# A four-layer transformer chain on one core: waiting for each part of a product's input instead of for all four

## The reference

```python
# L0: adaptive RMS norm, rotary attention (8 query heads of 64, one key/value head), silu-gated MLP of 2048
h = ada_rms(x, time_emb, ln1_w, ln1_tw); x = res + ctx @ Wo.T
h = ada_rms(x, time_emb, ln2_w, ln2_tw); x = res + silu(h @ Wg.T) * (h @ Wu.T) @ Wd.T
# L1: layer norm with scale and shift, cosine attention (16 heads of 32), gelu MLP of 2048
x = x + attn(_ln(x) * (scale1 + 1.0) + shift1) * gamma1
x = x + (gelu((_ln(x) * (scale2 + 1.0) + shift2) @ Wfc1.T + bfc1) @ Wfc2.T + bfc2) * gamma2
# L2: layer norm, sparse masked attention with a 128-wide latent for keys and values
out = y @ Wo.T; x = x + out
# L3: 8 expert MLPs (64 -> 256 -> 64), layer norm, silu, 512x512 product
proj = silu(hn) @ out_W + out_b; return x + proj
```

## Time and profile before

| | |
|---|---|
| median of 3 runs | 2081.14 us (2078.93 to 2084.55) |
| the profiled execution | 2079.02 us, span 2077.1 us |
| PE busy | 1904.8 us, 92% |
| DVE, ACT, POOL busy | 1114.6, 1027.6, 790.3 us |
| PE's granted clock, mean | 0.965 of 2.4 GHz |
| moved by DMA | 314.84 MB, mean 152 GB/s |

### The profile page before, as it was taken

How to read it: one execution, slowest core, us unless ns; L and a number is a source line. 1 busy time by engine, 2 the same in 40 slices (tenths; PEclk the granted TensorE clock), 3 DMA queues, 4 the chain that set the end, 5 groups by cost and what they waited for, 6 DMA issues and landing times.

```text
span 2077.1 us, 35268 instructions
## 1 busy us (share of the span) xinstructions
PE 1904.8 (92%) x12880; PEld 1507.4 (73%) x12880; DVE 1114.6 (54%) x3184; ACT 1027.6 (49%) x2473; POOL 790.3 (38%) x1094
## 2 busy tenths in 40 slices
PE   4789999999999999999899999989999989978977
PEld 3567777888778878887778777868876768755565
DVE  5756444644553365345664676574554675456353
ACT  3543323433343354443555465555567466368665
POOL 4555652211114242234667454326332432233220
PEclk9999999999999999999999999989999989989989
DMA  7235767555445445444345434523434425322311
GB/s 265 89 127 193 239 223 266 200 193 188 162 163 178 158 139 178 158 145 165 129 171 185 152 127 138 184 102 113 152 112 142 157 77 187 128 77 69 120 62 51
DMA packets 98795, 314.84 MB, mean 152 GB/s; under 512 B 11584, under 2 KB 13376, under 8 KB 97088
## 3 DMA queue, kind: packets, MB, share of 16 engines
q1 hardware_dynamic: 98624, 312.58, 43.9%
HBM read 242.55 MB, written 66.58 MB: 149 GB/s over the span
## 4 chain that ended last, share of the span: by engine, by line
PE 73%; DVE 12%; POOL 5%; ACT 5%; issue 4%; DMA 2%; SPq 0%; POOLq 0%; DVEq 0%; ACTq 0%
PE B L190 67%; PE B L193 6%; POOL R L208 2%; DVE FB L211 2%; DVE T L208 2%; DMA ST<-in_wpack 2%; DVE SS L214 1%; ACT FB L196 1%; ACT SS L196 1%; POOL W L208 1%; DVE PT L202 1%; POOL SS L205 1%; DVE FB L208 1%; DVE HA L211 1%; DVE Y L208 1%
## 5 line engine op out<-in xcount | busy, mean ns | idle before, releaser
L205 POOL TENSOR_SCALAR SS<-SS,NM 128x256 f32<-128x256 f32 (+1 forms) x640 | 289.0, 469 | 778.1 <-DVE NM L220 777.8
L190 PE MATMUL B<-HM,W 128*128 128x512 f32 x2304 | 538.3, 394 | 14.7 <-DVE HM L211 8.5
L190 PEld LDWEIGHTS B<-HM,W 128*128 128x128 f32 x2304 | 437.1, 190 | 108.6 <-DVE HM L211 9.4
L190 PE MATMUL B<-G,W 128*128 128x512 f32 x1536 | 394.9, 407 | 17.7 <-DVE G L208 6.0
L190 PEld LDWEIGHTS B<-G,W 128*128 128x128 f32 x1536 | 287.6, 193 | 88.4 <-issue 18.3
L196 ACT ACTIVATE SS<-SS,NM 128x256 f32<-128x256 f32 (+1 forms) x512 | 240.5, 471 | 117.1 <-DVE NM L214 116.5
L190 PE MATMUL B<-HA,W 128*128 128x512 f32 x864 | 222.1, 408 | 11.9 <-DVE HA L208 7.7
L193 PE MATMUL B<-ident,SS 128*128 128x128 f32 x1152 | 177.3, 291 | 36.6 <-POOL SS L205 30.7
L190 PEld LDWEIGHTS B<-HA,W 128*128 128x128 f32 x864 | 166.1, 196 | 49.6 <-DVE HA L208 8.1
L208 DVE TENSOR_TENSOR G<-FB,G 128x512 fp32r<-128x512 f32 x128 | 100.8, 788 | 171.9 <-ACT G L196 171.8
L193 PEld LDWEIGHTS B<-ident,SS 128*128 128x128 f32 x1152 | 128.2, 146 | 72.6 <-issue 44.5
(11 more groups left out here) (108 smaller groups left out, 2651.0 us busy)
## 6 DMA issues: line engine op xcount, KB each, us to landing
W<-kept SPq DMA_DIRECT2D x357, 512.0 KB, 4.2
kept<-W SPq DMA_DIRECT2D x119, 512.0 KB, 4.7
ST<-in_wpack SPq DMA_DIRECT2D x139, 256.0 KB, 2.9
Y<-in_adaw SPq DMA_DIRECT2D x12, 1024.0 KB, 5.9
FB<-FB SPq DMA_DIRECT2D x52, 64.0 KB, 3.0
X<-in_xT SPq DMA_DIRECT2D x1, 3072.0 KB, 14.4
out_xT<-X SPq DMA_DIRECT2D x12, 256.0 KB, 2.1
FB<-in_pos SPq DMA_DIRECT2D x4, 256.0 KB, 4.3
```

The source lines that it names most:

```text
L190: return self.real.matmul(*a, **k) if self.real is not None else self
L205: return self.real.tensor_scalar(*a, **k) if self.real is not None else self
```

## The change

`product` gets an argument `due`. Where it is given, the wait for part i of the input stands right before the three matmuls that read part i. It is given for the attention projections that read HA (the values of layer 1 at L1055 and the products from L2's latent keep theirs), for all `up`, `down` and last products. The waits for weights and bank stay ahead of the first matmul. Two numbers of `PLACE` change as well: the end of MLP 7 and the position of `nsub` in norms with a mean.

```diff
-    "up end": [35.49, 52.243, 66.359, 84.262, 100.699, 123.295, 147.706, 164.324],
+    "up end": [35.49, 52.243, 66.359, 84.262, 100.699, 123.295, 147.706, 163.582],
...
-    "a stats": [0.101, 1.202, 1.481, 1.791, 2.6],
+    "a stats": [0.101, 1.202, 1.42, 1.791, 2.6],
...
-            def product(bank, parts):
+            def product(bank, parts, due=None):
+
+
                 last = len(parts) - 1
                 for i, (w, x) in enumerate(parts):
+                    if due is not None:
+                        e.wait_ge(*due[0].of(*due[1:], i))
                     e.matmul(bank, w[0], x[0], start=(i == 0), stop=False)
...
-                        e.wait_ge(*d_nlo.of(("a", L, n), 3))
+                        due = d_nlo, ("a", L, n)
                     e.wait_ge(*ready(n, *name))
                     e.wait_ge(*dp.over(u))
-                    product(bank[:, :], parts).then_inc(*p_qkv.up(*k))
+                    product(bank[:, :], parts, due).then_inc(*p_qkv.up(*k))
...
-                    e.wait_ge(*d_nlo.of(("m", L, n), 3))
...
-                                                  for kc in range(4)]).then_inc(*p_up.up(q, c, j, x))
+                                                  for kc in range(4)], (d_nlo, ("m", L, n))).then_inc(*p_up.up(q, c, j, x))
...
-                        e.wait_ge(*d_glo.of(q, c, j))
...
-                                              for j in range(4)]).then_inc(*p_down.up(q, c, m))
+                                              for j in range(4)], (d_glo, q, c)).then_inc(*p_down.up(q, c, m))
...
-                    e.wait_ge(*d_nlo.of(("z", h, n), 3))
...
-                                               for c in range(4)]).then_inc(*p_last.up(n, m, h))
+                                               for c in range(4)], (d_nlo, ("z", h, n))).then_inc(*p_last.up(n, m, h))
```

More of the change, by code:

```diff
@@ L1006, in tensor @@
                         w, latent = piece(n, *name), piece(n, *LATENT)
-                        parts = [(part(w, 0, 128), latent)]
+                        parts, due = [(part(w, 0, 128), latent)], None
                         e.wait_ge(*d_ck.of(n))
```

## The result

The changed kernel takes 2062.62 us (median of 4 runs, 2061.08 to 2065.75); the kernel before, run beside it, 2082.85 us (4 runs, 2078.93 to 2085.32). The ratio is 0.9909, 95% interval 0.9889 to 0.9928: faster by 0.9%, some 20 us. The forecast was 2065 with a range of 2055 to 2077. The profiled executions lie 13.2 us apart (spans 2077.1 and 2063.9), since the one of before was near its fastest run and this one is the slowest of its four.

A forecast was written before the change was run, and what follows sets the result against it. PE, busy 1904.8 of 2077.1 us, was taken as the bound. Waits by part (19.8 us) plus places (1.0) made 20.8, times 0.8 gave 16.6 us won: forecast 2065 us, range 2055 to 2077.

The forecast's parts named there:

- What bounds the kernel, and the arithmetic of the gap: PE bounds; nine of twelve matmuls move into a gap, minimum 0.229 us each; idle falls 15 to 20 us.
- The six long waits: PE's six longest waits: 11.0 to 20.7 us won, middle 15.8; lower if the clock rises unchanged, upper if earlier.
- G at 218.57: PE's 2.37 us wait for G nearly closes, its product comes near 3 us: 2.1 to 3.8 us won.
- The two locks by bank: At ("a", 2, 3) and ("z", 2, 2) the first product also awaits its bank: 1.9 to 3.5 and 1.5 to 3.2 us.
- The nine short waits: PE's nine waits of 0.3 to 0.9 us mostly vanish: 3.5 to 4.7 us won, 4.0 taken.
- The places: Moved steps at MLP 7's end, chunks 2 and 3 and some norms: about +1 us together, bounds -3 and +4.
- How much arrives: Share of the 20.8 us reaching the kernel's end: between half and everything, factor 0.8 taken, 16.6 us.
- A: Clock comes back early in all six gaps and the places give their upper bound: 2056 us, chance 0.15.
- B: Bursts of matmuls leave the clock where it was, or it swings: 2069 us, chance 0.16.
- C: Gaps come back downstream, half or less of the gain arrives: 2071 to 2076 us, chance 0.17.
- D: Gaps filled but found again before the next squares or roots, places cost 3 us: 2081 to 2084, chance 0.06.
- E: Each of 171 waits inside products holds back the next load of weights: 2069 to 2097 us, chance 0.04.

The follow-up runs named there:

- eleven traces with four steps: Traces of the changed kernel and variants that wait separately for each of four input parts; the ten kernels' ratios lie between 0.9874 and 0.9910.
- places only: Kernel before with the two new `PLACE` numbers but the old waits: 2080.4 us, ratio 0.9985.
- the three traces of the table: Two traces of the changed kernel and one of the kernel before with waits by part but old places (2061.5 us, ratio 0.9893).
- the second trace: Another trace of the unaltered changed kernel, against the kernel before: 13.4 us gained over all matmuls.
- the end alone: Changed kernel with `nsub` put back at its old position, so waits by part and the new MLP 7 end: 2060.62 us, ratio 0.9899.
- the two kernels with the cover kept: Changed kernel with old `nsub` position and MLP 7 end at 164.1; one also waits for `down` weight pieces by part: 2059.15 and 2060.36 us.
- the second measurement of the two kernels: Changed kernel run again, unaltered, as yardstick against the kernel before on one chip: 2058.72 us, ratio 0.9881.
- the two-step kernel: Changed kernel with parts 0 to 2 all waiting for part 2 and part 3 for itself: 2067.08 us, ratio 0.9912.

## Why the prediction was right, point by point

**What bounds the kernel, and the arithmetic of the gap: right.** PE's idle time fell by 17.0 us where 15 to 20 were forecast; over the eleven traces with four steps it is 150.1 to 159.3 us, 13 to 22 less. The waits left by name are 7.5 us; with the two that the bank now ends (2.5 at ("a",2,3) and 4.6 at ("z",2,2)) they are 14.6, at the low end of the 14 to 20.

**The six long waits: right in sum, wrong in two of its terms.** 3.6 + 3.4 + 1.1 + 2.6 + 1.2 + 1.5 = 13.4 us against a middle of 15.8, inside 11.0 to 20.7. Its lower bound, 0.229 per moved matmul, rested on the clock rising at the same moment as before. It did not: at ("m",0,0) nothing behind the last part was left at the lower clock, so that gap gave its upper bound, in all eleven traces with four steps. At ("a",0,0) seven or eight matmuls moved, as forecast, and the gain was mostly over the upper bound of 3.1 (2.6 to 4.4 us in these traces; 0.7 in places only, where nothing moved, is the noise of such a figure). Where the pauses stay (("m",1,0)) the clock rose 1.3 us sooner, and the gap gave 2.6, 1.5 and 2.0 us, about its lower bound of 2.1, in the three traces of the table; over all eleven it is 1.4 to 3.6, and more where the clock came back sooner. So both bounds were met in this gap, and what decides between them from one execution to the next is open. The terms below their lower ends are G at 218 us and ("a",2,3), next.

**G at 218.57: right where it arises, wrong downstream.** The product came to 2.96 us as forecast and 3.2 us were won, in the range of 2.1 to 3.8. But 1.1 (or -0.6 in the second trace) are left at 230 us. The step that failed is "all other waits of PE (softmax rows, sums of squares, reciprocal roots, weights, banks) stay as they are": a wait for weights that had been hidden behind the wait for G came out two steps later.

**The two locks by bank: right.** The first product behind ("a",2,3) and ("z",2,2) starts with the bank, not with part 0. PE of the changed kernel, with releasers that are the scalings, as the earlier trace rows said:

```profile
1837.05 4.57 PE L190 MATMUL B<-HA,W 128*128 128x512 f32 x12 [2.47 <-DVE FB L211]
...
1982.50 0.77 PE L190 MATMUL B<-ZH,W 128*128 128x512 f32 x1 [4.63 <-DVE FB L208]
```

These two gave 1.2 and 1.5 us, below and at their lower ends (1.9 and 1.5): behind the bank nearly all of the product is at the lower clock (4.57 us for 12, 4.36 before). That is not so in every order: with the end alone and in the two kernels with the cover kept, ("a",2,3)'s product takes 3.0 us and the gap gives 2.5; in the other eight traces it gives 1.1 to 1.7.

**The nine short waits: right.** The five that I can follow singly gave 1.0, 1.1, 1.0, 0.6 and about 0.8 us (1670 to 1690), 4.5 together, where 4.0 were forecast for all nine. One of them, at 165 us, was lost again: `few,T` and the scores behind it then waited 0.19 and 1.95 us (the latter 1.41 before).

**The places: inside the bounds, but with the wrong sign.** +1 forecast, with bounds of -3 and +4; in the trace -1.2 at ("a",2,0), +1.2 at `nvar`, +1.2 at chunk 3 and about -2.7 behind it, some -1.5. The first is as forecast. At `nvar` only the idle time counts: the kernels that leave `nvar` where it was gained 1.5 there too. The product behind it takes 4.20 us in the trace of before and 3.0 in all five others that have it there, so the share of the clock was not the place's. The term that was missing is the last one. The working had asked what the moved steps meet at their new place, and not what stood at the place they left: a 3 us `down` that covered a softmax. That accounts for 1.1 us of it; the rest is the slow product behind. By the medians the places are worth nothing either way. This is the sort of step that one has to look for in the order.

**How much arrives: not confirmed.** Of the 20.8 us of the sum 16.6 were to arrive. It was 13.2 in the profiled pair, 20.2 in the medians, and 27.2 in the medians of the second measurement of the two kernels, which is over the whole sum. The range held all of these; the factor 0.8 fits neither median. The factor was to stand for DVE not following; what took gain away in the traces are weights at 190 to 230 us, the softmax rows at 1810 us, and spells of low clock which differ by 4 us and more from one execution to the next. In those the pair of traces is misleading: PE's busy time is 1902.1 to 1911.1 us in kernels that do the same matmuls.

**The rivals.** A (2056) is half there: the clock came early in the gap that closed, not in those with pauses. B (2069) is out as an account of the whole: the first two gaps gave more than their lower bounds (3.6 and 3.4 against 1.7), and the bursts beat the single start of the two-step kernel. Its lower bounds held at ("z",2,2) and nearly at ("m",1,0). C is true of single gaps (165, 212 us) and not of the whole. D and E are out: idle time fell and did not come back, and waits cost nothing that shows. E's range was also summed wrongly: 20 to 32 us on top of 2064.5 are 2085 to 2097, not 2069 to 2097. Of the signs named, the mean clock does not rise in the profiled pair (0.964, where it was 0.965), but that execution of before is near the top of its kind. Over 35 executions of before in the experiments the mean is 0.961 (0.956 to 0.966), and on one chip 0.961 against 0.966 in six of the changed kernel. So the sign came, and single traces hide it.

What stays open: why the spells fall where they do. The one at some 760 us is in four of fourteen traces, all with the new position of `nsub`, but in four others with that position it is absent, and it was not tried to provoke it.

## What to carry over

Wait for each part of an operand where it is read, not for the whole ahead of the product: no cost of the extra waits shows when they are met, and what moves into the gap is worth something from its time at full clock to about twice that (nine matmuls, 2.1 us at full clock, gave 1.4 to 3.6 us in one and the same gap). Before you count the gain, find what else the product's first instruction waits for (its bank, its weights) and what the next few products wait for, since a gain of 3 us can be gone two products later. When steps are moved, look at the place that they leave: a filler between a softmax and its reader is cover, even if it waits for nothing itself.

## What was not expected of the hardware

The granted clock's row does not tell everything at the start of the program. Twelve matmuls from 26.39 us of before took 4.59 us at a granted 1.00, while ten of the same took 4.31 at 0.50 elsewhere and twelve take some 2.75 at full clock. The first of the changed kernel, from 22.88 us, step at 0.43 us and more as well, and a little later, at the same granted 1.00, it is ten in 2.00 us:

```profile
28.00:30.00 2.00, 2.00 (x10) 1.66 (x9) 0.00 (x0) 1.23 (x3) 0.00 (x0) 1.00 0.96 325
```

And bursts of three matmuls between pauses did not hold the clock: it fell in the middle of the bursts at ("m",1,0) (0.54 in the slice 994 to 996), yet it returned 1.3 us sooner than without them, and 0.1 to 3.3 us sooner in the eleven traces that have them.
